# Attention scores on TensorE: from two 64-row tiles to four 32-row tiles, with another order of blocks

## The reference

```python
Q = jax.nn.relu(queries @ Wq + bq)      # (16, 100, 128)
K = jax.nn.relu(keys @ Wk + bk)         # keys = values = ctx, (16, 1444, 128)
V = jax.nn.relu(values @ Wv + bv)
scores = jnp.einsum('hbqd,hbkd->hbqk', Qh, Kh) * scale     # scale = 1 / 8 ** 0.5
scores = jnp.where(key_mask[None, :, None, :] == 0.0, NEG, scores)
attn = jax.nn.softmax(scores, axis=-1) * q_mask[None, :, :, None]
out = jnp.einsum('hbqk,hbkd->hbqd', attn, Vh)
return out.transpose(1, 2, 0, 3).reshape(B, Sq, D) + queries
```

## Time and profile before

| | before |
|---|---|
| median of 3 runs | 408.71 us (408.44 to 408.76) |
| profiled execution | 409.39 us |
| its span | 407.6 us |
| TensorE matmuls busy | 389.7 us, 96% |
| weight loads busy | 265.1 us, 65% |
| ScalarE busy | 305.4 us, 75% |
| VectorE busy | 231.0 us, 57% |
| GpSimd busy | 14.1 us, 3% |
| chain that ended last | TensorE 87%, VectorE 6% |
| value products, L523 | 158.5 us, 340 ns each |
| scores, L508 | 121.5 us, 289 ns each |
| exponentials, L434 | 293.2 us, 840 ns each, idle before them 83.7 us |

### The profile page before, as it was taken

The page is one execution under the profiler, slowest core; times in us unless marked ns, Lnnn a source line. Parts: engine busy times, 40 slices in busy tenths (PEclk is TensorE's granted clock), DMA queues, the critical chain, the costliest instruction groups (busy, mean ns, idle before and its releaser), DMA issues.

```text
span 407.6 us, 13727 instructions
## 1 busy us (share of the span) xinstructions
PE 389.7 (96%) x5216; PEld 265.1 (65%) x5216; DVE 231.0 (57%) x717; ACT 305.4 (75%) x408; POOL 14.1 (3%) x25
## 2 busy tenths in 40 slices
PE   7889699999999999999999999999999988999995
PEld 5756357675767667575767667575766656667663
DVE  1968756473838466473847557473847554366111
ACT  2687548787878787787878787787887864787993
POOL 9400000000000000000000000000000000000000
PEclk9999989999999999999999999999999996999999
DMA  7783616362634526172543616172543615025000
GB/s 238 193 288 154 224 55 238 104 253 87 242 126 163 205 91 238 57 278 73 227 141 149 219 73 242 53 290 78 212 156 136 232 54 226 21 93 209 7 7 8
DMA packets 20960, 62.52 MB, mean 153 GB/s; under 512 B 4938, under 2 KB 10954, under 8 KB 20938
## 3 DMA queue, kind: packets, MB, share of 16 engines
q1 hardware_dynamic: 20218, 61.32, 40.3%
q10 hardware_dynamic: 720, 0.89, 0.7%
HBM read 13.73 MB, written 0.82 MB: 36 GB/s over the span
## 4 chain that ended last, share of the span: by engine, by line
PE 87%; DVE 6%; issue 3%; POOL 2%; ACT 1%; DVEq 0%; ACTq 0%; POOLq 0%
PE psum L523 35%; PE psum L508 26%; PE psum L466 13%; PE psum L461 11%; PE psum L472 2%; POOL selectors L363 2%; DVE k_raw L731 1%; ACT probs L434 1%; DVE k_cent L745 1%; DVE v_biased L767 1%; DVE values L774 1%; DVE k_high L745 1%; DVE q_sum L885 1%; DVE k_parts L899 0%; POOL selectors L356 0%
## 5 line engine op out<-in xcount | busy, mean ns | idle before, releaser
L434 ACT ACTIVATE probs<-psum 128x800 f32<-128x800 f32 x384 | 293.2, 840 | 83.7 <-PE psum L508 83.7
L523 PE MATMUL psum<-probs,values 128*32 128x200 f32 x3072 | 158.5, 340 | 0.7 <-issue 0.7
L508 PEld LDWEIGHTS psum<-query_bd,k_parts 64*128 64x128 f32 x1536 | 97.5, 189 | 48.8 <-ACT probs L434 30.4
L523 PEld LDWEIGHTS psum<-probs,values 128*32 128x32 f32 x3072 | 87.6, 110 | 63.1 <-ACT probs L434 30.4
L508 PE MATMUL psum<-query_bd,k_parts 64*128 64x200 f32 x1536 | 121.5, 289 | 4.7 <-issue 3.0
L731 DVE TENSOR_SCALAR_CACHE_REDUCE k_raw<-psum,bk_sb 128x512 f32<-128x512 f32 (+1 forms) x48 | 34.4, 719 | 85.3 <-PE psum L461 85.2
L466 PE MATMUL psum<-wv_sb,keyT 128*128 128x129 f32 x384 | 59.8, 294 | 0.5 <-DVE v_biased L767 0.5
L461 PE MATMUL psum<-keyT,wk_mixed 128*128 128x512 f32 (+1 forms) x96 | 51.2, 618 | 3.8 <-DVE k_raw L731 3.8
L466 PEld LDWEIGHTS psum<-wv_sb,keyT 128*128 128x128 f32 x384 | 48.2, 193 | 7.3 <-DVE v_biased L767 0.8
L774 DVE TENSOR_SCALAR values<-v_biased,keep 128x128 f32<-128x128 f32 x192 | 43.4, 283 | 6.9
L767 DVE TENSOR_TENSOR v_biased<-psum,bv_sb 128x384 f32<-128x384 f32 x64 | 35.0, 547 | 0.0
(11 more groups left out here) (61 smaller groups left out, 96.6 us busy)
## 6 DMA issues: line engine op xcount, KB each, us to landing
k_parts<-k_high SPq DMA_DIRECT2D x120, 180.5 KB, 2.2
k_parts<-k_low SPq DMA_DIRECT2D x120, 180.5 KB, 2.2
keyT<-in_ctxT SPq DMA_DIRECT2D x15, 722.0 KB, 4.2
query_rep<-k_parts SPq DMA_DIRECT2D x16, 200.0 KB, 2.3
x_sb<-in_x SPq DMA_DIRECT2D x1, 800.0 KB
out<-x_sb SPq DMA_DIRECT2D x16, 50.0 KB
values<-in_xT ACTq DMA_DIRECT2D x1, 600.0 KB, 6.7
keyT<-in_ctxT SPq DMA_DIRECT2D x2, 256.0 KB, 4.0
```

What stands on the lines that cost most here:

```text
L434: nc.scalar.activation(probs[:, u % PROB_SLOTS], scores_ps[:, u % SCORE_SLOTS, :, 0:QCOLS], ACT.Exp, scale=SCALE).then_inc(probs_ready, 1)
L508: mm = nc.tensor.matmul(scores_ps[:, u % SCORE_SLOTS, j, n * TCOLS:(n + 1) * TCOLS], k_parts[rows, parity, t, kt * P:(kt + 1) * P], query_ ...
L523: mm = nc.tensor.matmul(o_ps[c * VCOLS:(c + 1) * VCOLS, half * PCOLS:(half + 1) * PCOLS], values[:, parity, kt, half * HALF_PAIRS + c, :], ...
```

## The change

**Tiles.** `TILE` is 32 instead of 64: a row tile holds one head, and needs no mask. `query_now` replaces `query_bd`: the queries once, 128 x 4 x 100, filled by one VectorE copy instead of four masked multiplications. `blockmask` and its semaphore go. A matmul has 32 rows and 100 moving columns; its weights are 128 columns as before. A unit's halves are now heads of the same quads: half 0 is the row tiles 0 and 1, half 1 the tiles 2 and 3, and each runs over all four quads `t`. So a unit has eight matmuls.

**Two units at once.** `scores` takes a range of units and goes by key tile. Where both halves of a key tile are among them, their matmuls are interleaved (per `t`, tiles 0, 1, 2, 3) after one wait for both slots. A cycle's three units are thus a pair and a single one, in turn one or the other first.

**Order.** A cycle's blocks are scores, value products, side work. On VectorE, the second centring (`k_cent`) opens the next batch instead of closing this one, the low keys come after the first value group, and the copy of a batch's sums follows the transposes of the batch before at the end of `batch`. At the start, units 0 and 1 are scored together and wait for all four value groups.

```diff
-TILE = 64
+TILE = 32
...
-        query_bd = sb("query_bd", [P, 2, QUADS, TCOLS], F32R)
+        query_now = sb("query_now", [P, 2, QUADS, SQ], F32R)
...
-                if not isinstance(b, int) or b > 0 or u >= SCORE_SLOTS:
-                    pe.wait_ge(probs_ready, UNITS * b + u + 1 - SCORE_SLOTS)
-                for n in range(HALF_QUADS):
-                    t = half * HALF_QUADS + n
-                    for j in range(TILES):
-                        rows = slice(j * TILE, (j + 1) * TILE)
-                        mm = nc.tensor.matmul(scores_ps[:, u % SCORE_SLOTS, j, n * TCOLS:(n + 1) * TCOLS],
-                                              k_parts[rows, parity, t, kt * P:(kt + 1) * P],
-                                              query_bd[rows, parity, t, :], start=True, stop=True)
-                mm.then_inc(scores_ready, 1)
+                for kt in range(units[0] // HALVES, units[-1] // HALVES + 1):
+                    halves = tuple(h for h in range(HALVES) if HALVES * kt + h in units)
+                    u = HALVES * kt + halves[-1]
+                    if not isinstance(b, int) or b > 0 or u >= SCORE_SLOTS:
+                        pe.wait_ge(probs_ready, UNITS * b + u + 1 - SCORE_SLOTS)
+                    for t in range(QUADS):
+                        for half in halves:
+                            for bank in range(HALF_QUADS):
+                                tile = half * HALF_QUADS + bank
+                                rows = slice(tile * TILE, (tile + 1) * TILE)
+                                mm = nc.tensor.matmul(
+                                    scores_ps[:, (HALVES * kt + half) % SCORE_SLOTS, bank, t * SQ:(t + 1) * SQ],
+                                    k_parts[rows, parity, t, kt * P:(kt + 1) * P],
+                                    query_now[rows, parity, t, :], start=True, stop=True)
+                            if t == QUADS - 1:
+                                mm.then_inc(scores_ready, 1)
...
-                        values[:, parity, kt, half * HALF_PAIRS + c, :],
-                        probs[:, u % PROB_SLOTS, tile, n * PCOLS:(n + 1) * PCOLS],
+                        values[:, parity, kt, HALVES * c + half, :],
+                        probs[:, u % PROB_SLOTS, :, c * SQ:(c + 1) * SQ],
...
+                    next_scores(range(units[0] + LEAD, units[-1] + LEAD + 1))
                     for u in units:
-                        next_scores(u + LEAD)
+                        value_products(b, parity, u)
                     for step in side[cycle][-1:]:
                         side_work(step)
...
-                    for u in units:
-                        value_products(b, parity, u)
...
                 if c == KCHUNKS - 2:
-                    first_scores(0)
+                    pe.wait_ge(first_evacuated, KCHUNKS + VGROUPS)
+                    scores(0, 0, range(0, EARLY_UNITS))
...
-                for t in range(QUADS):
-                    ins = v.tensor_tensor(
-                        query_bd[:, parity, t, :].rearrange("p (h q) -> p h q", h=TILE_HEADS),
-                        src[:, t].bitcast(F32).unsqueeze(1).to_broadcast([P, TILE_HEADS, SQ]),
-                        blockmask[:].unsqueeze(2).to_broadcast([P, TILE_HEADS, SQ]), ALU.mult)
-                ins.then_inc(qbd_ready, 1)
+                v.tensor_copy(query_now[:, parity], src.bitcast(F32)).then_inc(query_ready, 1)
...
-                center_keys(k_cent, parity, k_cent_ready)
...
-            def batch(b, parity, last=False, keys=True):
+            def batch(b, parity, keys=True):
                 used = works_before(b)
-                copy_outputs(b - 1)
-                if last:
-                    finish_outputs(b - 1, used)
-                    return used + 1
-                finish_keys(b + 1)
+                center_keys(k_cent, 1 - parity, k_cent_ready)
                 for g in range(VGROUPS):
                     finish_values(b + 1, 1 - parity, g, used + g)
                     if g == 0:
+                        finish_keys(b + 1)
+                    elif g == 1:
                         spread_queries(b + 1, 1 - parity)
...
+                dve.wait_ge(work_filled, used + 1)
+                copy_outputs(b)
                 finish_outputs(b - 1, used)
```

64 lines of the change are left out of this document (24 added, 40 removed).

## The result

| | before | after |
|---|---|---|
| median of the timed executions | 408.57 us (408.16 to 408.76) | 438.45 us (433.24 to 443.44, 4 of them) |
| profiled execution | 409.39 us | 433.77 us |
| its span | 407.6 us | 432.0 us |

The change makes the kernel **slower by 6.1%**: the ratio is 1.061, with an interval of 1.0587 to 1.0633.

The account below looks back on a forecast made before the run. TensorE, busy throughout, was taken as the bound. Score blocks 20.5, late cycles 1.0, batch 0 to 1 boundary 1.1, start-up 3.1 and half clock 1.3 sum to 27.0 us on 408.71: 435.7 us, range 425 to 455.

Parts of the forecast that it names:

- The score block: TensorE's scores each cycle: eight rounds of weight loads in place of six, 0.85 to 1.03 us, 114 times, 20.5 us.
- Its reason: Score block: a pair takes four rounds, the single unit four more with two tiles empty, eight at 0.11 us each.
- Order of the blocks in the steady stretch: Scores, products, work in the loop: costs nothing; the output copy at a batch's end is hidden with 0.2 us to spare.
- The +1.1 us of the prediction: Between batch 0 and 1: cycle 7's products, 1.15 us, leave the wait and stand ahead of the key projection.
- Start-up: First scores wait for the last value group; first exponential at 27.6, cycle 1 3.1 us later, plus 1.3 us half clock.
- Batch 0: Four of its cycles pay 0.18 us each; no added half clock beyond the earlier trace's 3.4 us after a 3.83 us wait.
- The loop's exit: TensorE's 3.2 us wait there, likely an instruction fetch; the sum has no term for it changing.
- rival (c): Loop no longer stays on the chip: six waits of 3.2 us plus half clock, +28, 464 us; chance 0.05.
- Late cycles: Nine last cycles with scores but no work, set by the exponentials: between 0 and 1.6 us, taken as 1.0 us.
- (a): Score block: loads over 32 rows are quick, the stream sets the round; 24 us faster, 384.6 us; chance 0.08.
- (b): Score block: four row tiles don't load side by side; +0.62 us a block, 488 us; chance 0.04.
- (d): TensorE's clock falls more often as score blocks stream less; a tenth of the span at 1.2 GHz, 455 us; chance 0.03.

Follow-up runs that it names:

- doubled matmuls: Changed kernel with each score matmul of a half-0 unit (row tiles 0 and 1) issued twice, same result: 489.14 us, one execution.
- the kernel with both edits: Changed kernel with VectorE's reductions over the queries moved into gaps of batch 0 and unit 0's scores issued early in the start-up: 423.00 us, ratio 1.034.
- the 400.67 us kernel: Kernel before with 20 one-element matmuls inserted in batch 0 and VectorE's two query reductions moved to two later gaps: 400.67 us, ratio 0.979.
- 200 columns: Changed kernel with 200 moving columns for each score matmul in place of 100, same weight loads and scores: 435.54 us, ratio 1.063.
- early unit: Changed kernel with unit 0's scores alone issued once value groups 0 to 3 are evacuated, units 1 and up later: 427.63 us, ratio 1.050.

## Why the prediction was right, and where it wasn't

The forecast of 435.7 us stands 2.2 us above the 433.5 that it is compared with; its main terms hold, and errors of 4.0 and 6.3 us in it cancel in part. That the sum came so near is luck in this respect.

- **The score block: right in size.** +0.18 us forecast, 1.02 for 0.85 measured, 0.18 a cycle in the steady stretch. Load time independent of rows, four tiles abreast, and the halved last matmul (0.04 forecast, 0.05 with the columns restored) each have a run or a row.
- **Its reason: half wrong.** "Two tiles stand empty while the single unit runs ... and nothing of another unit can shorten that" holds only because the busy tiles have eight loads each. The count is by tile and not by rounds in program order. From rounds in program order, 485 us were expected for the kernel without pairing; the run gave 430.
- **Order of the blocks in the steady stretch: right**, nothing. The boundary's copy is hidden from batch 2 on. At the boundary of batch 0 the wait is 0.80 us in after, TensorE having run at half clock up to it; the other kernels with this order, but for the one with doubled matmuls (1.40), waited 1.60 to 1.82 us there, where before's wait was 0.69. The +1.1 us of the prediction is borne out: from the last products of batch 0 to the first of batch 1, 4.80 us in the kernel with both edits (51.94 to 56.74) against 3.63 in the 400.67 us kernel (52.42 to 56.05).
- **Start-up: 4.4 forecast with its half clock, 3.0 measured, and otherwise made up.** The step "the last value group, which VectorE evacuates at 24.51" failed: after had it at 22.93, and the first exponential at 25.86, not 27.6. The rows are below. The half clock that the prediction put on the last eight selections, after a wait from 21.2 to 24.6, didn't come: they ran at full clock from 23.57. Two other stretches took the gain back, 1.6 us each; with neither, and with unit 0 early, cycle 1 began at 28.40, earlier than before's 29.69.
- **Batch 0: missed, +4.0 us.** The prediction left the half clock there as the earlier trace rows had it, 3.4 us. It was 17.1 us, and why so long stays open.
- **The loop's exit: missed, -6.3 us.** The wait of 3.2 us was in the earlier trace rows and I used it only as a price for rival (c). I left it in the sum as if after would have it too: "nothing" for the exit was a choice not stated. Here such a wait, for "issue" and explained by no engine, went away when 80 instructions were inserted, and it went away with a change that adds 384 loads and matmuls to each pass.
- **Late cycles: 1.1 us short.** Score blocks there take 1.16 to 1.29 us in after's chain (402.65, 404.99), against 1.00 to 1.08 in before's: the pair's common release does show, more than the 1.0 us I took.
- **The rivals.** (a) quick 32-row loads, (b) two abreast: out by the block of 1.02 us. (c): after keeps its loop on the chip, and where a loop isn't kept it cost no wait, so the price was wrong too. (d): the clock did fall more often, for 23.9 us ahead of the end where before had 10.2, but in the start-up and batch 0, never in the steady stretch.

The Trainium skill (TensorE: Matmul & The Clock Gate, "LDWEIGHTS") gives a load's cost by its columns whatever its rows. The trace agrees over 32 rows: 0.11 us a round. Its section on packing small matmuls, which spoke for this change, gives a speed-up measured at 512 moving columns. No run here has that shape; at 100 and 200 columns, the runs show that the load sets the round and that four tiles of 32 rows do no more work in a turn than two of 64.

The start-up's rows, timeline of before and then of after, GpSimd's fills beside VectorE's two centring passes:

```profile
12.92 0.71 POOL L382 MEMSET k_parts<- 128x736 f32 x1
12.97 1.43 DVE L745 TENSOR_SCALAR k_high<-k_raw,k_max 128x1444 fp32r<-128x1444 f32 x1
...
14.00 1.64 POOL L385 MEMSET values<- 128x1440 f32 x1 [0.36 <-PE psum L600]
...
14.32 2.08 DVE L745 TENSOR_SCALAR k_cent<-k_raw,k_max 128x1444 f32<-128x1444 f32 x1
```

```profile
12.17 0.71 POOL L373 MEMSET k_parts<- 128x736 f32 x1
...
12.97 0.97 DVE L731 TENSOR_SCALAR k_high<-k_raw,k_max 128x1444 fp32r<-128x1444 f32 x1
...
13.86 0.97 DVE L731 TENSOR_SCALAR k_cent<-k_raw,k_max 128x1444 f32<-128x1444 f32 x1
```

Both begin at 12.97. Before's take 3.51 us beside two fills, after's take 1.94 beside none. The 1.57 us between them is what the last value group came early by. I had put the removed masks down at nothing. They are behind the first pass: their fills push the one at 12.92 back by 0.75 us, into it, and in the kernel with the order alone, which keeps the masks, it took 1.43 us again, beside a fill at 12.95. The second pass there took 0.95 us, since its fill came at 15.70; in after it comes at 15.69. That fill waits for TensorE's query projection, and both kernels ran that at half clock. With the tiles alone, the projection at full clock and no masks, the second pass began at 13.87, ahead of the fill at 14.01, and took 0.96 us. (That the fills are what stretches the passes is read from these traces; no run changes the fills alone.)

## To carry to other kernels

Before a matmul is cut into smaller row tiles, count the weight loads on the busiest tile: with short streams these set the time. Here 12 loads in a cycle, six on each of two tiles, became 24, eight on each of two tiles and four on each of the others. A pair of units has four rounds for two units, as many as before; by this count the price is that of the odd third unit, and a cycle with an even number of units would neither lose nor gain a round. No run tests that. Where the profile shows a wait for "issue" that no engine explains, at a loop's exit above all, try shifting the program by some tens of instructions placed in existing idle time; here it was worth 4.9 us, and it can add to or hide the effect of any change that alters the program's length. And take out waits of a few us on TensorE even where they look affordable, since half clock behind them can cost more than they do: in before, moving two reductions by one gap each was worth 3.2 us here.

## What the runs showed of the hardware

- **Row tiles run on independently of program order.** Three units issued one behind the other took the 1.02 us of the interleaved ones, with 24 loads in 0.97 us and four matmuls started in the first 0.05 us; 32 loads spread evenly took 0.99 us, 40 unevenly 1.86 us.
- **Half clock isn't in proportion to the wait at it.** Behind the wait for VectorE's keys in batch 0, TensorE worked at the 1.2 GHz level for 3.4 us after 3.83 us of waiting (before) and after 2.87 (with 20 matmuls), for 4.5 us after 3.65 (tiles alone; the level fell 2.4 us ahead of the wait's end), for 6.4 us after 2.98 (order alone), for 6.8 us after 2.76 to 2.80 (units in program order, 200 columns, early unit, doubled matmuls), and for 17.1 us after 2.80 in after. Behind 7.85 us of inserted waits it was 5.65 us. At the first products of batch 1, waits of 1.60 to 1.82 us went with 3.4 us in five kernels and with 6.8 in one, and a wait of 1.40 us with none. With waits of 0.82, 0.46 and 0.68 us alone it never fell. What decides between these lengths stays open.
- **A wait instruction on TensorE isn't free**: 80 instructions that only waited for a semaphore long since there took 7.85 us in one kernel and 7.83 in another.
- **Instructions fetched in each pass of a loop cost no wait** at some 16 KB every 6 us (72 blocks). Fetches at a loop's exit went with 3 us of waiting in before and with none in the kernel with 20 inserted matmuls.
